# Gated delta-rule layer on one Trainium2 core: residuals from three bf16 pieces, and a new order of fillers

## The reference, cut to what matters

```python
def step(state, inp):
    q_t, k_t, v_t, b_t, d_t = inp
    state = state * d_t[..., None, None]
    Sk = jnp.einsum('bhi,bhij->bhj', k_t, state)
    delta = (v_t - Sk) * b_t[..., None]
    state = state + jnp.einsum('bhi,bhj->bhij', k_t, delta)
    o = jnp.einsum('bhi,bhij->bhj', q_t, state)
    return (state, o)
```

## Time and profile before

| | us |
|---|---|
| median of 3 runs | 1804.15 |
| lowest, highest | 1802.18, 1804.24 |
| the profiled execution | 1804.3 |
| its span, first to last instruction | 1802.3 |
| PE busy | 1703.3 (95%) |
| DVE busy | 1316.0 (73%) |
| ACT busy | 1167.9 (65%) |
| POOL busy | 652.5 (36%) |
| mean granted PE clock | 0.982 |

### The profile page before, as it was taken

One profiled execution on the slowest core, in us unless ns is written; L12 is line 12 of the kernel. 1 busy time (PEld: TensorE's weight loads), 2 busy tenths in 40 slices (PEclk: granted clock), 3 DMA queues, 4 the chain that ended last, 5 costly groups with the idle time before them and its releaser, 6 DMA issues.

```text
span 1802.3 us, 34261 instructions
## 1 busy us (share of the span) xinstructions
PE 1703.3 (95%) x13208; PEld 1322.5 (73%) x13208; DVE 1316.0 (73%) x2293; ACT 1167.9 (65%) x2185; POOL 652.5 (36%) x474
## 2 busy tenths in 40 slices
PE   7899999999998987999999999999999999999986
PEld 5676766767665666787787787877877877878875
DVE  7788888888866267767768767777677687677753
ACT  3335353443535465778878878887787788788762
POOL 2222213222214063615516426336246165163340
PEclk9999999999999997999999999999999999999998
DMA  3111010101103200110110101101101201111000
GB/s 138 35 55 47 33 67 33 67 33 55 46 1 105 76 19 1 37 59 25 37 56 28 36 25 60 36 25 37 59 25 36 60 25 36 38 47 36 7 2 24
DMA packets 51447, 75.16 MB, mean 42 GB/s; under 512 B 3392, under 2 KB 41792, under 8 KB 51312
## 3 DMA queue, kind: packets, MB, share of 16 engines
q1 hardware_dynamic: 51312, 73.28, 12.6%
HBM read 72.03 MB, written 1.25 MB: 41 GB/s over the span
## 4 chain that ended last, share of the span: by engine, by line
PE 54%; ACT 7%; DVE 6%; issue 3%; DVEq 0%
PE bank L731 12%; PE bank L911 7%; PE bank L751 5%; PE bank L866 4%; PE bank L789 3%; PE bank L802 2%; PE bank L816 2%; PE bank L812 2%; DVE d_sil L1334 2%; ACT d_dec L1133 2%; PE bank L874 2%; PE bank L887 2%; PE bank L854 2%; PE bank L888 2%; PE bank L889 2%
## 5 line engine op out<-in xcount | busy, mean ns | idle before, releaser
L1634 POOL TENSOR_TENSOR d_dec<-d_dec,d_qk 128x384 f32<-128x384 f32 x128 | 138.8, 1111 | 638.4 <-DVE d_N L1359 571.3
L1334 DVE SCALAR_TENSOR_TENSOR d_sil<-d_pre,d_w,d_sil 128x1024 f32<-128x1024 f32 x192 | 295.2, 1538 | 10.1 <-ACT d_pre L1099 9.9
L731 PE MATMUL bank<-xnT,d_w 128*128 128x512 f32 x480 | 242.4, 617 | 0.0
L189 PE MATMUL bank<-xnT,a_w 128*128 128x512 f32 x512 | 236.6, 596 | 0.0
L1380 DVE CAST_PREDICATED d_X<-tables_sb,bank 128x512 bf16<-128x512 int32 x192 | 134.3, 700 | 89.9 <-PE bank L802 76.4
L1396 DVE TENSOR_TENSOR d_Rb<-d_V,bank 128x512 bf16<-128x512 f32 x128 | 86.5, 685 | 109.8 <-PE bank L866 109.8
L489 POOL TENSOR_TENSOR a_hidc<-a_hid,a_comb 128x512 f32<-128x512 f32 x32 | 44.4, 1387 | 295.0 <-DVE a_hid L336 295.0
L189 PEld LDWEIGHTS bank<-xnT,a_w 128*128 128x128 f32 x512 | 90.6, 192 | 78.5 <-issue 78.5
L1161 ACT ACTIVATE d_T<-bank 128x512 bf16<-128x512 f32 x160 | 100.5, 628 | 65.2 <-PE bank L812 62.6
L866 PE MATMUL bank<-d_W,d_N 128*128 128x128 f32 x1024 | 130.6, 281 | 2.0 <-DVE d_W L1401 1.9
L508 ACT ACTIVATE a_sg<-a_sm 128x384 f32<-128x384 f32 x64 | 33.0, 515 | 152.0 <-DVE a_sm L341 152.0
(11 more groups left out here) (210 smaller groups left out, 4274.8 us busy)
## 6 DMA issues: line engine op xcount, KB each, us to landing
d_dec<-decay_scratch SPq DMA_DIRECT2D x32, 512.0 KB, 5.7
a_w<-w SPq DMA_DIRECT2D x16, 897.0 KB, 4.6
d_w<-w SPq DMA_DIRECT2D x16, 776.0 KB, 4.6
a_comb<-comb_scratch SPq DMA_DIRECT2D x16, 512.0 KB, 5.6
d_dec<-decay_scratch SPq DMA_DIRECT2D x32, 256.0 KB, 6.1
d_wo<-w SPq DMA_DIRECT2D x16, 256.0 KB, 3.1
f_w<-w SPq DMA_DIRECT2D x8, 256.0 KB, 4.2
x_sb<-x SPq DMA_DIRECT2D x2, 512.0 KB, 4.4
```

The source lines that it names most:

```text
L189: last = pe.matmul(psum[bank][:, :], wq(slot, part, k), xnT[:, k, half * HALF:(half + 1) * HALF], start=(k == 0), stop=(k == KT - 1))
L731: last = pe.matmul(psum[bank][:, :], cols(slot, (c * KT + k) * P, P), xnT[:, k, h * HALF:(h + 1) * HALF], start=(k == 0), stop=(k == KT - 1))
L1334: dve.scalar_tensor_tensor(sil[c][:, :, :], pre[c % 2][:, :, tap:tap + S], cols(slot, OC + 4 * c + tap, 1), sil[c][:, :, :], ALU.mult, ALU ...
L1634: pool.tensor_tensor(g, g, qk[b][:, :, :], ALU.mult).then_inc(s["p_done"], 1)
```

## The change

The matrix blocks of N (planes 0 and 2) are split into three bf16 pieces that add up to the fp32 values: `Nh` (rounded by ACT, `high`), `Nm` and `Nl` (POOL, `middle` and `lowest`). W is kept as a bf16 first part `W0b` and a bf16 correction `dWb`. `residual` then is two bf16 matmuls a block for a = 0 (Nh and Nm by W0b) and three for a = 1 (Nl by W0b, Nh and Nm by dWb), accumulated in the bank over both rounds. `apply` no longer accumulates. POOL adds W0b and dWb (`partial`), and DVE adds the last correction from PSUM (`total`) for both value heads. POOL's mask is issued in two halves, one before the split, one after it and before `partial`. Of the fillers, `project_out` is issued in half quarters: its first two quarters in the inversion, the last two in rounds k = 1 and 2 of the solve; the next head's projections, gate and norms move later. `behind` becomes `inner`, which stands between the two value heads' residuals.

```diff
+        Nh = [m.sb(f"d_Nh{v}", [P, B, 2, P], BF16) for v in range(2)]
+        Nm = [m.sb(f"d_Nm{v}", [P, B, 2, P], BF16) for v in range(2)]
+        Nl = Nb
+        W0b = [m.sb(f"d_W0b{v}", [P, B, P], BF16) for v in range(2)]
+        dWb = [m.sb(f"d_dWb{v}", [P, B, P], BF16) for v in range(2)]
...
                     last = pe.matmul(psum[4 + 2 * v][:, b * P:(b + 1) * P], TT[v][:, 2 * b + c, :], Rb[v][:, b, :],
-                                     start=(a == 0 and b == 0), stop=(a == 2), skip_group_check=True)
+                                     start=True, stop=True)
...
             def residual(i, v, c, a):
                 if a == 0:
                     pe.wait_ge(s["w0_done"], i * 4 + 2 * c + v + 1)
-                    pe.wait_ge(s["diag_done"], i * 2 + v + 1)
+                    pe.wait_ge(s["nm_done"], i * 2 + v + 1)
+                    parts = ((Nh, W0b), (Nm, W0b))
                 else:
-                    pe.wait_ge(s[f"wup_done{v}"], i * 4 + 2 * c + a)
-                for b in range(B):
-                    last = pe.matmul(psum[5 + 2 * v][:, b * P:(b + 1) * P], N[v][:, b, 2 * c, :], Wv[v][:, b, c, :],
-                                     start=True, stop=True)
+                    pe.wait_ge(s["nl_done"], i * 2 + v + 1)
+                    pe.wait_ge(s[f"dw_done{v}"], i * 2 + c + 1)
+                    parts = ((Nl, W0b), (Nh, dWb), (Nm, dWb))
+                for n, (coef, vec) in enumerate(parts):
+                    for b in range(B):
+                        last = pe.matmul(psum[5 + 2 * v][:, b * P:(b + 1) * P], coef[v][:, b, c, :], vec[v][:, b, :],
+                                         start=(a == 0 and n == 0 and b == 0), stop=(a == 1 and n == 2), skip_group_check=True)
                 last.then_inc(s["resid_ready"], 1)
...
             def link(i, v):
-                pe.wait_ge(s[f"wup_done{v}"], i * 4 + 2)
+                pe.wait_ge(s[f"wup_done{v}"], i * 2 + 1)
...
-            def project_out(j, slot, i, n, nxt=None):
+            def project_out(j, slot, i, n, nxt=None, parts=(0, 1)):
...
-                for q in range(2):
+                for q in parts:
...
-                last.then_inc(s["out_ready"], 1)
+                if 1 in parts:
+                    last.then_inc(s["out_ready"], 1)
...
-                    for n, (li, half) in enumerate(((3, 1), (4, 0), (4, 1), (5, 0))):
-                        fill[li][half].append(lambda n=n: project_out(*before, n, nxt))
...
-                ahead, between, behind, closing = ([[] for _ in range(6)] for _ in range(4))
+                    out = lambda n, q: (lambda: project_out(*before, n, nxt, (q,)))
+                    fill[3][1].append(out(0, 0))
+                    fill[4][0].append(out(0, 1))
+                    fill[4][1].append(out(1, 0))
+                    fill[5][0].append(out(1, 1))
+
...
+                ahead, between, inner, closing = ([[] for _ in range(6)] for _ in range(4))
...
-                    for c, h, li, half in ((2, 0, 2, 1), (2, 1, 3, 0), (3, 0, 5, 1)):
-                        fill[li][half].append(p(c, h))
+                    for h, (li, half) in enumerate(((2, 1), (3, 0))):
+                        fill[li][half].append(p(2, h))
+                    fill[5][1].append(part(3, 0, 0))
...
-                    ahead[0], between[0], behind[0] = [part(3, 1, 0)], [part(3, 1, 1)], [z(0, 0)]
-                    between[1], behind[1] = [z(0, 1)], [q(0, 0)]
-                    between[2], behind[2], closing[2] = [q(0, 1)], [q(1, 0)], [q(1, 1)]
-                    between[3] = [z(1, 0)]
-                    between[4] = [z(1, 1)]
+                    ahead[0], between[0], inner[0] = [part(3, 0, 1)], [part(3, 1, 0)], [part(3, 1, 1)]
+                    closing[2] = [q(0, 0), q(0, 1)]
+                    between[3], inner[3] = [z(0, 0)], [q(1, 0), q(1, 1)]
+                    between[4], inner[4] = [z(0, 1)], [z(1, 0)]
+                    closing[5] = [z(1, 1)]
+                if not (isinstance(i, int) and i == 0):
+                    between[1], inner[1] = [out(2, 0)], [out(2, 1)]
+                    between[2], inner[2] = [out(3, 0)], [out(3, 1)]
...
-                        for f in behind[k]:
-                            f()
                         for v in range(2):
                             if a < 2:
                                 residual(i, v, c, a)
                             elif c == 0:
                                 link(i, v)
+                            if v == 0:
+                                for f in inner[k]:
+                                    f()
                         for f in closing[k]:
...
+            def high(i, v):
+                act.wait_ge(s["diag_done"], i * 2 + v + 1)
+                act.activation(Nh[v][:, :, :, :], N[v][:, :, 0:3:2, :], ACT.Copy).then_inc(s["nh_done"], 1)
+
             def first_w(i, v, c):
                 act.wait_ge(s["apply_ready"], i * 12 + 6 * c + v + 1)
-                act.activation(Wv[v][:, :, c, :], psum[4 + 2 * v][:, :].rearrange("p (b d) -> p b d", b=B),
+                act.activation(W0b[v][:, :, :], psum[4 + 2 * v][:, :].rearrange("p (b d) -> p b d", b=B),
                                ACT.Copy).then_inc(s["w0_done"], 1)
...
-            def next_w(i, c, a):
-                act.wait_ge(s["apply_ready"], i * 12 + 6 * c + 2 * a + 1)
-                act.activation(Wv[0][:, :, c, :], psum[4][:, :].rearrange("p (b d) -> p b d", b=B),
-                               ACT.Copy).then_inc(s["wup_done0"], 1)
+            def change(i, c):
+                act.wait_ge(s["apply_ready"], i * 12 + 6 * c + 3)
+                act.activation(dWb[0][:, :, :], psum[4][:, :].rearrange("p (b d) -> p b d", b=B),
+                               ACT.Copy).then_inc(s["dw_done0"], 1)
...
+                for v in range(2):
+                    fill[4][v].append(lambda v=v: high(i, v))
...
-                next_w(i, 0, 1)
...
-                    batch_decays(ni, ns, 1)
-                next_w(i, 0, 2)
-                if nxt:
-                    batch_decays(ni, ns, 2)
                 for v in range(2):
...
                 if nxt:
+                    batch_decays(ni, ns, 1)
+                change(i, 1)
+                if nxt:
+                    batch_decays(ni, ns, 2)
                     batch_decays(ni, ns, 3)
-                next_w(i, 1, 1)
-                if nxt:
                     silu(ni, 2)
-                next_w(i, 1, 2)
-                if nxt:
                     silu(ni, 3)
...
-            def update(i, c, a):
-                dve.wait_ge(s["apply_ready"], i * 12 + 6 * c + 2 * a + 2)
-                dve.tensor_copy(Wv[1][:, :, c, :], psum[6][:, :].rearrange("p (b d) -> p b d", b=B)).then_inc(s["wup_done1"], 1)
+            def change(i, c):
+                dve.wait_ge(s["apply_ready"], i * 12 + 6 * c + 4)
+                dve.tensor_copy(dWb[1][:, :, :], psum[6][:, :].rearrange("p (b d) -> p b d", b=B)).then_inc(s["dw_done1"], 1)
+
+            def total(i, v, c):
+                dve.wait_ge(s["apply_ready"], i * 12 + 6 * c + 4 + v + 1)
+                dve.wait_ge(s["wsum_done"], i * 4 + 2 * c + v + 1)
+                dve.tensor_tensor(Wv[v][:, :, c, :], Wv[v][:, :, c, :], psum[4 + 2 * v][:, :].rearrange("p (b d) -> p b d", b=B),
+                                  ALU.add).then_inc(s[f"wup_done{v}"], 1)
...
                 if not first:
-                    for n, (li, h) in enumerate(((4, 0), (4, 1), (5, 0), (5, 1))):
-                        fill[li][h].append(lambda n=n: add_out(i - 1, n))
+                    for n in range(2):
+                        fill[4 + n][1].append(lambda n=n: add_out(i - 1, n))
+                        end[2 + n].append(lambda n=n: add_out(i - 1, 2 + n))
                 if nxt:
-                    fill[5][0].append(cv(2, 0))
-                    mid[0], end[0] = [cv(2, 1)], [cv(2, 2)]
-                    mid[1], end[1] = [cv(3, 0)], [cv(3, 1)]
-                    mid[2] = [cv(3, 2)]
-                    end[3] = [lambda: guard(ns, ni)]
+                    fill[4][0].append(cv(2, 0))
+                    fill[5][0].append(cv(2, 1))
+                    mid[0].append(cv(2, 2))
+                    mid[1].append(cv(3, 0))
+                    end[1].append(cv(3, 1))
+                    mid[2].append(cv(3, 2))
+                    end[3].append(lambda: guard(ns, ni))
...
-                        if a:
-                            update(i, c, a)
+                        if a == 1:
+                            change(i, c)
+                        elif a == 2:
+                            for v in range(2):
+                                total(i, v, c)
...
+            def diagonal(i, v):
+
+                pool.wait_ge(s["nb_done"], i * 2 + v + 1)
...
+            def middle(i, v):
+
+                pool.wait_ge(s["nh_done"], i * 2 + v + 1)
+                rest = N[v][:, :, 0:3:2, :]
```

(28 more changed lines are left out.)

32 lines of the change are left out of this document (16 added, 16 removed).

## The result

The changed kernel takes 1886.59 us (median of 4 runs, 1885.75 to 1888.83) against 1803.16 for the kernel before (4 runs): ratio 1.0467, 95% interval 1.0449 to 1.0485. The profiled execution took 1888.83; its span is 1887.1, against 1802.3 before: 84.8 us more.

A forecast was written before the change was run, and what follows sets the result against it. PE's work was taken to bound the kernel before; afterwards POOL's chain delays `link`: 14 x (5.7 + 1.35) = 99 us, less 10 for heads 0 and 15, on 1804.3 gives 1893 us. Range 1820 to 1945.

The forecast's parts named there:

- T, the end of the second partial sum: POOL's chain, from head start H: H + 32.0, 19.4 us work, 5.6 us collisions, ending at H + 57.0.
- The residuals on PE: Residual matmuls on PE: 7.4 us a head in fp32 become 4.6 in bf16, so PE sheds 2.8.
- POOL's prices: POOL's new list: two-input instructions of 1024 elements at 2.35 us, 1.90 as lower side; 19.4 us in all.
- Collisions: POOL's new stretch beside DVE's convolution steps: six collisions at 0.94 us each, 5.6 us a head.
- PE at `link`: PE reaches `link` at H + 47.7, then stands idle most of 9 us in pieces, some 3 ahead of `link`.
- the one on fillers: Moved fillers cost PE zero; displaced ACT and DVE steps 0 to 1 us a head, taken as 0.
- Rival 1: POOL's new instructions run at a copy's rate: T at H + 50.4, no clock loss, 1782 us; chance 0.10.
- From T to the next head, and the clock: Work behind T takes 19.1 us; a lower clock after the wait adds 0 to 2.7, taken as 1.35.
- Heads 0 and 15: Head 0, with `f_tail` behind the last `partial`, nets -8 us; the last head, without mask or convolutions, -2.
- (2): Collisions beside POOL's list largely fail to occur, two of six: +2.6 us a head, 1831 us; chance 0.14.
- (3): Clock stays low from `link` to the outputs: 6 us more a head, 1977 us; chance 0.06.
- (4): The split sheds nothing on PE, waits only move; POOL's chain gives the forecast's time, so no separate chance.

The follow-up runs named there:

- e5: Changed kernel with three DVE convolution steps of channel group 3 cut to 8 columns in every head but the first (output changes): 1849.55 us, ratio 1.0247.
- e3: Kernel before, keeping its fp32 arithmetic and POOL list, with the change's order of fillers and DVE's moved convolutions and additions: 1851.83 us, ratio 1.0264.
- e1: Changed kernel with POOL's masks moved behind chunk 0's partial sums and ACT's decays behind its last bf16 change: 1828.61 us, ratio 1.0142.
- e7: e6 with two of POOL's three `f_tail` steps in head 0 moved ahead of the masks and chunk 1's partial sums: 1828.87 us, ratio 1.0147.
- e6: e1 with two norm halves of PE work moved ahead of `link` and ACT's first squares behind its bf16 change: 1829.88 us, ratio 1.0153.
- e9: e3 with the two norm halves of PE work placed ahead of `link`: 1850.75 us, ratio 1.0278.
- e10: e1 with two DVE convolution steps moved out of chunk 0 and ACT's SiLU of two channel groups moved into the solve: 1801.07 us, ratio 0.9993.
- e12b: e10 with one more DVE convolution step moved from ahead of chunk 0's second `left_over` to behind its totals: 1790.07 us, ratio 0.9932.
- e8: Changed kernel with two norm halves of PE work moved from behind `link` to ahead of it: 1866.88 us, ratio 1.0356.

## Why the prediction was right

It said 1893 and the time is 1886.6. The reason it gave, POOL's chain setting `link`, is the one that the trace and e5 show. That the number came so near is in part luck: two of its errors, 17 us too much in the heads and 13 too little at the ends, nearly cancel. By its own steps:

- **T, the end of the second partial sum.** Predicted H + 57.0, measured H + 55.4, in one unbroken row of POOL work from the diagonal on, which ends at H + 32.0 as it did before.
- **The residuals on PE.** 4.6 us a head predicted. In the head at 1264.66 a residual of two pieces takes 0.45 us and one of three 0.67, 4 x 1.12 = 4.5 in all.
- **POOL's prices.** Two inputs over 1024 elements: 2.35 predicted, 2.12 to 2.13 measured. POOL's own work comes to 5.0 (masks) + 6.3 (middle) + 4.2 (lowest) + 2.3 (partial) = 17.8 where 19.4 stood. The nearest cheaper row, 1.90, was as near as the one taken, and both bounds held. The Trainium skill's rule (GPSIMD Engine Reference, Elementwise — side-by-side cycle accounting), about 2.6 cycles an element for two inputs, gave an estimated 2.2 us for 1024 elements at 1.2 GHz. The trace agrees, with 2.13 where the second input is bf16, and 1.15 for 512 with both inputs in bf16.
- **Collisions.** Six at 0.94, 5.6 in all. Measured: two in the first masks (4.46 - 2.50), one in each copy (1.91 and 1.92 for 1.04), one in the second masks and one in the partial sums: six, 5.7 us. e5 took two of them away and got 0.97 for each. The strict reading of the Trainium skill's lock (SBUF — State Buffer, Who interferes with whom) would have been 1.28; no run shows that.
- **PE at `link`.** Predicted H + 47.7, measured 1319.82 - 3.09 = H + 52.1. The step that failed is the one on fillers: it bounded the cost of the order and of the displaced ACT and DVE steps by 0 to 1 us a head. e3 shows 3.2. It did no harm to the number because the same step said that POOL's wait would cover it, and it did: 9.3 us of idle PE were forecast ahead of T. T came 1.6 earlier, 4.4 went to shorter waits ahead of `link`, and 3.1 were left at `link`. The prediction put those shorter waits down to POOL's pieces; only one of 0.4 us is for such a piece, the others are for DVE's and ACT's work. Rival 1 would have been mispriced, though. It put T at H + 50.4 and the time at 1782. e1 has T at H + 51.0 and took 1829, on the other side of the old time.
- **From T to the next head, and the clock.** Predicted 19.1 + 1.35 = 20.45, measured 1341.04 - 1320.09 = 20.95. The granted clock is 0.72 around `link`, and `link`'s second half, 3.5 us after the first, takes its usual 1.05 us; the first half and the half quarter behind it take 1.87 and 1.59 us from start to start where e1, at full clock, has 0.99 and 0.87, a loss of 1.6. Over the three kinds of heads the loss is 0, 1.6 and 2.8, 1.5 on average. The middle of 0 to 2.7 was taken with no row to decide it, and met the average by luck; no head has it. Without a dip T to the next head is 19.3, against 19.1.
- **The period.** 5.7 + 1.35 = 7.05 a head predicted, 5.85 measured; 14 x 1.2 = 17 us too much.
- **Heads 0 and 15.** Predicted -8 and -2. Head 2 starts 807.2 - 797.9 = 9.3 us later than before, 5.8 of it a period's, so head 0 is 3.5 us longer (1.4 by its end, the rest behind it, where the transposes take 3.65 us for 1.91 at the lower clock); the last head takes 88.7 us (1887.1 - 1798.4), as before (1802.3 - 1713.6). This was wrong in sign: the step counted what `f_tail` gives back to the convolutions and too little of what it takes from the gating. e7, built on e6, shows that the two are nearly equal. The error of 13 us here hides most of the 17 above.

The rivals: (1) is out by the 2.13; (2) by six collisions of six; (3) by the clock, which was back at or soon behind the second half of `link` (longest loss 2.8 us a head); (4), that the split sheds nothing on PE, is out too, since PE's busy time fell by 8 us, although e3, which has the order alone, has 12 us more of it (1714.9) than before.

## What to carry to other kernels

When work is shifted from the full engine to one that looks free, don't ask for the free engine's share but for the place in its list where the new chain must start, and for who waits for its end; then put behind that chain whatever of the list nobody awaits (e1: 58 us for moving POOL's masks and ACT's decays). Fillers are no cost-free mass: a filler shortened from 1.8 to 0.9 us uncovers what stands beside it in the other engines' lists, and a long wait elsewhere can hide that until it is removed. When a wait only changes its place as cover is moved (e6, e9), shorten the list of the engine that is waited for (e10, e12b).

## What the runs showed of the hardware

Both sides pay for a collision of POOL and DVE. A copy (1.91 for 1.04), a pair of masks and a pair of sums each became 0.87 to 0.98 us longer by one convolution step. That step, 1.28 us alone, takes 2.3 to 2.95 in the four rows above, and 1.90 on average in the changed kernel against 1.54 in the one before.

The granted clock isn't a fixed price of a wait. In the changed kernel the same wait of 3.1 us ahead of `link` is followed in turn by no dip (a head of 74.8 us), by one that costs 1.6 us and by one that costs 2.8. In e8, with 1.31 us, 4 heads of 14 have a dip and 10 have none; in e1, with 1.7 us, none has. What decides between them was not tried. For whoever reads one head of a trace, it means that a second and a third are to be looked at before its length is taken for the period.
